# The first adjacency block of the first gather, loaded and multiplied in two column halves

## The reference

```python
def L0(x, adj, W):
    deg = sum(adj, axis=-1, keepdims=True)
    agg = einsum('bij,bjf->bif', adj, x) / maximum(deg, 1e-6)
    return relu(einsum('bnf,of->bno', concatenate([x, agg], 2), W))

def L1(X, A, kernel, bias):
    Ah = A + eye(1024)
    dh = rsqrt(sum(Ah, axis=-1))
    An = dh[:, :, None] * Ah * dh[:, None, :]
    return relu(einsum('bnm,bmf,fc->bnc', An, X, kernel) + bias)

x = layernorm(x + L0(x, adj, L0_gnn_W))
x = layernorm(x + L1(x, adj, L1_gnn_kernel, L1_gnn_bias))
```

## Time and profile before

| | |
|---|---|
| median of three runs | 500.82 us (500.78 to 501.29) |
| the profiled execution | 501.08 us, of which the span from first to last instruction is 499.3 us |
| TensorE busy | 490.4 us, 98% of the span, 2751 matmuls |
| VectorE, ScalarE busy | 393.2 us (79%), 330.6 us (66%) |
| DMA | 93.38 MB, mean 187 GB/s |

### The profile page before, as it was taken

How to read it: one execution, slowest core, us unless ns; L and a number is a source line. 1 busy time by engine, 2 the same in 40 slices (tenths; PEclk the granted TensorE clock), 3 DMA queues, 4 the chain that set the end, 5 groups by cost and what they waited for, 6 DMA issues and landing times.

```text
span 499.3 us, 8174 instructions
## 1 busy us (share of the span) xinstructions
PE 490.4 (98%) x2751; PEld 430.4 (86%) x2751; DVE 393.2 (79%) x963; ACT 330.6 (66%) x614; POOL 2.3 (0%) x8
## 2 busy tenths in 40 slices
PE   8999999999999999999999999999999999999993
PEld 7988888988899888998889988898888988889993
DVE  6787897679966799667996679866898668976755
ACT  6898557765766658756596574965848658477415
POOL 0000000000000000000000000000000000000001
PEclk9999999999999999999999999999999999999998
DMA  8999509762195523936149280593607932051002
GB/s 306 398 376 394 200 1 347 286 210 86 56 376 199 210 84 100 390 140 243 52 155 388 94 287 0 196 393 107 227 0 258 372 120 90 0 211 43 0 1 84
DMA packets 36878, 93.38 MB, mean 187 GB/s; under 512 B 2944, under 2 KB 3840, under 8 KB 36864
## 3 DMA queue, kind: packets, MB, share of 16 engines
q1 hardware_dynamic: 36432, 92.81, 51.1%
q10 hardware_dynamic: 432, 0.39, 0.3%
HBM read 84.80 MB, written 8.39 MB: 187 GB/s over the span
## 4 chain that ended last, share of the span: by engine, by line
PE 97%; ACT 1%; DMA 1%; DVE 0%; POOL 0%; issue 0%; DVEq 0%; ACTq 0%
PE ring_b L890 22%; PE ring_b L892 22%; PE ring_b L891 22%; PE ring_a L890 9%; PE ring_a L892 9%; PE ring_a L891 9%; PE ring_b L936 1%; PE ring_b L945 1%; PE ring_b L949 1%; DMA adj_raw<-adjT 1%; ACT x L381 0%; ACT adj_nat L498 0%; ACT adj_nat L495 0%; POOL x L307 0%; DVE x L678 0%
## 5 line engine op out<-in xcount | busy, mean ns | idle before, releaser
L890 PE MATMUL ring_b<-adj_hi,x1s_hi 128*128 128x512 f32 (+1 forms) x256 | 98.3, 384 | 0.0
L892 PE MATMUL ring_b<-adj_hi,x1s_lo 128*128 128x512 f32 (+1 forms) x256 | 98.0, 383 | 0.0
L891 PE MATMUL ring_b<-adj_lo,x1s_hi 128*128 128x512 f32 (+1 forms) x256 | 97.9, 382 | 0.0
L890 PE MATMUL ring_b<-adj_hi,x_hi 128*128 128x512 f32 x240 | 93.7, 391 | 0.0
L892 PE MATMUL ring_b<-adj_hi,x_lo 128*128 128x512 f32 x240 | 93.5, 390 | 0.0
L891 PE MATMUL ring_b<-adj_lo,x_hi 128*128 128x512 f32 x240 | 93.3, 389 | 0.0
L313 ACT ACTIVATE gath_hi<-ring_b 128x512 fp32r<-128x512 f32 (+1 forms) x64 | 36.5, 583 | 64.5 <-PE ring_b L892 64.5
L547 DVE TENSOR_TENSOR adj_lo<-adj_raw,adj_hi 128x1024 fp32r<-128x1024 f32 (+1 forms) x68 | 76.4, 1158 | 3.1 <-ACT adj_hi L313 3.1
L328 ACT ACTIVATE adj_nat<-adj_nat 128x1024 f32<-128x1024 f32 x64 | 67.2, 1052 | 4.9 <-DMA adj_nat<-adjN 4.6
L313 ACT ACTIVATE adj_hi<-adj_raw 128x1024 fp32r<-128x1024 f32 (+2 forms) x68 | 65.0, 997 | 1.8 <-DMA adj_raw<-adjT 1.7
L547 DVE TENSOR_TENSOR gath_lo<-ring_b,gath_hi 128x512 fp32r<-128x512 f32 (+1 forms) x64 | 42.6, 678 | 21.7 <-ACT gath_hi L313 21.7
(11 more groups left out here) (112 smaller groups left out, 966.2 us busy)
## 6 DMA issues: line engine op xcount, KB each, us to landing
adj_nat<-adjN SPq DMA_DIRECT2D x64, 512.0 KB, 5.8
adj_raw<-adjT SPq DMA_DIRECT2D x60, 512.0 KB, 9.2
out<-x SPq DMA_DIRECT2D x15, 512.0 KB, 3.3
xt_raw<-xT SPq DMA_DIRECT2D x7, 1024.0 KB, 4.8
x_sb<-x SPq DMA_DIRECT2D x14, 512.0 KB, 4.8
adj_raw<-adjT SPq DMA_DIRECT2D x8, 256.0 KB, 5.3
x_sb<-x SPq DMA_DIRECT2D x3, 256.0 KB, 5.3
x<-w SPq DMA_DIRECT2D x2, 256.0 KB, 6.3
```

The costliest lines, as they stand in the source:

```text
L890: nc.tensor.matmul(o, lhi, rhi, start=(first and i == 0), stop=False)
L891: nc.tensor.matmul(o, lhi, rlo, start=False, stop=False)
L892: last = nc.tensor.matmul(o, llo, rhi, start=False, stop=last_part)
```

## The change

The load of piece 0 is cut into a left and a right load of 256 columns each, with a semaphore each. x tile 0 goes from the head of ScalarE's queue to the head of SP's queue. x tiles 2 and 3 (the pair i = 1) go from SP's queue to ScalarE's. On ScalarE the activation table load is issued ahead of its two loads instead of behind them. VectorE casts x tile 0 and forms its remainder first and casts the right half of piece 0 afterwards. PE runs 14 warm-up matmuls; block 0's first two pairs are eight matmuls of 256 columns, four on the left half, then four on the right half, and each side waits for its own rounded half. The start flag is given with the left side's first matmul of each bank only. The pair with a_lo stays at 512 columns.

```diff
--- before.py
+++ after.py
@@ -19,7 +19,7 @@
 NB = 4
 NR = 4
 XP = 2
-WARM = 15
+WARM = 14
 LINE = 128
 HALF = LINE // 8
 PART = (slice(0, NH // 2), slice(NH // 2, NH))
@@ -113,6 +113,7 @@
         x0_loaded = sem("x0_loaded")
         x0_hi_done, x0_lo_done = sem("x0_hi_done"), sem("x0_lo_done")
         adj0_left_hi, adj0_right_hi = sem("adj0_left_hi"), sem("adj0_right_hi")
+        adj0_right_loaded = sem("adj0_right_loaded")
         x_first_hi, x_first_lo = sem("x_first_hi"), sem("x_first_lo")
         adj_first_hi, adj_first_lo = sem("adj_first_hi"), sem("adj_first_lo")
         x_hi_done, x_lo_done = sem("x_hi_done"), sem("x_lo_done")
@@ -227,11 +228,14 @@
                 sp.wait_ge(out_done, b * H + h + 1)
                 sp.dma_start(x_half(out[b], h), x_half(x1, h)).then_inc(x1_free[h], 16)
 
-            sp.dma_start(raw[:, 0, 0, :], adjT[0, 0, 0]).then_inc(raw_first_loaded[0], 16)
+            sp.dma_start(x_sb[:, 0, :], x_first[0]).then_inc(x0_loaded, 16)
+            sp.dma_start(raw[:, 0, 0, 0:NH // 2], adjT[0, 0, 0, :, 0:NH // 2]).then_inc(raw_first_loaded[0], 16)
+            sp.dma_start(raw[:, 0, 0, NH // 2:NH], adjT[0, 0, 0, :, NH // 2:NH]).then_inc(adj0_right_loaded, 16)
             sp.dma_start(raw[:, 0, 1, :], adjT[0, 0, 1]).then_inc(raw_loaded[0][0], 16)
             for i in range(1, CH):
-                loaded = x_first_loaded[i // 2] if i % 2 == 0 else x_loaded[i // 2]
-                sp.dma_start(x_pair(x_sb, i).rearrange("p t c -> p (t c)"), x[0, i]).then_inc(loaded, 16)
+                if i > 1:
+                    loaded = x_first_loaded[i // 2] if i % 2 == 0 else x_loaded[i // 2]
+                    sp.dma_start(x_pair(x_sb, i).rearrange("p t c -> p (t c)"), x[0, i]).then_inc(loaded, 16)
                 sp.dma_start(raw[:, 0, JC * i, :], adjT[0, 0, JC * i]).then_inc(raw_first_loaded[i], 16)
                 sp.dma_start(raw[:, 0, JC * i + 1, :],
                              adjT[0, 0, JC * i + 1]).then_inc(raw_loaded[0][i], 16)
@@ -499,9 +503,9 @@
                                      bias=shift16[:, q:q + 1],
                                      accum_out=moments[:, q, 1:2]).then_inc(act_var_done, 1)
 
-            act.dma_start(x_sb[:, 0, :], x_first[0]).then_inc(x0_loaded, 16)
+            nc.scalar.preload_act_table(ACT.Sqrt)
             act.dma_start(x_sb[:, 1, :], x_first[1]).then_inc(x_first_loaded[0], 16)
-            nc.scalar.preload_act_table(ACT.Sqrt)
+            act.dma_start(x_pair(x_sb, 1).rearrange("p t c -> p (t c)"), x[0, 1]).then_inc(x_loaded[0], 16)
             act.wait_ge(raw_first_loaded[0], 16)
             copy(adj_block(a_hi, 0, 0, 0, NH // 2), raw[:, 0, 0, 0:NH // 2]).then_inc(adj0_left_hi, 1)
             act.wait_ge(x_first_loaded[0], 16)
@@ -830,13 +834,13 @@
             nc.vector.memset(stats[:], 0.0).then_inc(x1_free[0], 16)
             nc.vector.memset(nb[:], 0.0).then_inc(x1_free[1], 16)
             nc.vector.memset(quarter_eps[:], LN_EPS / 4).then_inc(eps_ready, 1)
-            dve.wait_ge(raw_first_loaded[0], 16)
-            nc.vector.tensor_copy(adj_block(a_hi, 0, 0, NH // 2, NH // 2),
-                                  raw[:, 0, 0, NH // 2:NH]).then_inc(adj0_right_hi, 1)
             dve.wait_ge(x0_loaded, 16)
             nc.vector.tensor_copy(x_hi[:, 0, :], x_sb[:, 0, :]).then_inc(x0_hi_done, 1)
             dve.wait_ge(x0_hi_done, 1)
             minus(x_lo[:, 0, :], x_sb[:, 0, :], x_hi[:, 0, :]).then_inc(x0_lo_done, 1)
+            dve.wait_ge(adj0_right_loaded, 16)
+            nc.vector.tensor_copy(adj_block(a_hi, 0, 0, NH // 2, NH // 2),
+                                  raw[:, 0, 0, NH // 2:NH]).then_inc(adj0_right_hi, 1)
             dve.wait_ge(adj0_left_hi, 1)
             dve.wait_ge(adj0_right_hi, 1)
             minus(adj_block(a_lo, 0, 0, 0, NH), raw[:, 0, 0, :],
@@ -922,8 +926,6 @@
                     a_at, x_at = adj_block(a_hi, 0, j, 0, NH), x_hi[:, j, :]
                     if j == 0:
                         pe.wait_ge(x0_hi_done, 1)
-                        pe.wait_ge(adj0_left_hi, 1)
-                        pe.wait_ge(adj0_right_hi, 1)
                     elif j == 1:
                         pe.wait_ge(x_first_hi, 1)
                         pe.wait_ge(adj_hi_done, 1)
@@ -932,18 +934,28 @@
                         pe.wait_ge(adj_first_hi, i)
                     else:
                         pe.wait_ge(adj_hi_done, i + 1)
-                    for f in range(FT):
-                        nc.tensor.matmul(ring_b[:, f, :], x_at[:, f * P:(f + 1) * P], a_at,
-                                         start=(j == 0), stop=False)
                     if j == 0:
-                        pe.wait_ge(x0_lo_done, 1)
-                    elif j == 1:
-                        pe.wait_ge(x_first_lo, 1)
-                    elif j % JC == 0:
-                        pe.wait_ge(x_first_lo if j % TH == 0 else x_lo_done, j // TH + 1)
-                    for f in range(FT):
-                        nc.tensor.matmul(ring_b[:, f, :], x_lo[:, j, f * P:(f + 1) * P], a_at,
-                                         start=False, stop=False)
+                        for i0, side_hi in ((0, adj0_left_hi), (NH // 2, adj0_right_hi)):
+                            side, a_side = slice(i0, i0 + NH // 2), adj_block(a_hi, 0, 0, i0, NH // 2)
+                            pe.wait_ge(side_hi, 1)
+                            for f in range(FT):
+                                nc.tensor.matmul(ring_b[:, f, side], x_at[:, f * P:(f + 1) * P], a_side,
+                                                 start=(i0 == 0), stop=False)
+                            pe.wait_ge(x0_lo_done, 1)
+                            for f in range(FT):
+                                nc.tensor.matmul(ring_b[:, f, side], x_lo[:, 0, f * P:(f + 1) * P], a_side,
+                                                 start=False, stop=False)
+                    else:
+                        for f in range(FT):
+                            nc.tensor.matmul(ring_b[:, f, :], x_at[:, f * P:(f + 1) * P], a_at,
+                                             start=False, stop=False)
+                        if j == 1:
+                            pe.wait_ge(x_first_lo, 1)
+                        elif j % JC == 0:
+                            pe.wait_ge(x_first_lo if j % TH == 0 else x_lo_done, j // TH + 1)
+                        for f in range(FT):
+                            nc.tensor.matmul(ring_b[:, f, :], x_lo[:, j, f * P:(f + 1) * P], a_at,
+                                             start=False, stop=False)
                     pe.wait_ge(adj_first_lo if j % JC == 0 else adj_lo_done, i + 1)
                     for f in range(FT):
                         last = nc.tensor.matmul(ring_b[:, f, :], x_at[:, f * P:(f + 1) * P],
```

## The result

The changed kernel takes 502.06 us (median of 22 runs, 501.0 to 504.65) against 501.0 us of the kernel before (22 runs beside it, 500.48 to 501.64). The ratio is 1.0023, 95% interval 1.0015 to 1.0031. The median hides the shape: of the 22 runs of the changed kernel 11 lie between 501.0 and 501.8 and 11 between 502.3 and 504.7, with none in between. The kernel before has one group.

A forecast was written before the change was run, and what follows sets the result against it. TensorE, busy 98% of the span, was taken as the bound, so changes before block 1 pass to the end. Block 1 at 6.78 instead of 6.96 us gains 0.2 us: 500.6 us, range 500.2 to 501.8.

The forecast's parts named there:

- the same: Whole kernel: a time within about 0.2%, 1.0 us, of the kernel before; chance 0.85.
- the hold by the table load: ScalarE's start: the activation table load might delay the DMA issues behind it, by 0, 1.28 or at most 2.64 us.
- case B: Table load holds ScalarE's DMAs 1.28 us; PE starts at 4.5, block 1 at 6.78; 0.2 us gained, 500.6 us, chance 0.42.
- cases A, B and C: ScalarE's DMAs held not at all, 1.28 us, or up to 2.64 us: 501.2, 500.6, 501.7 us; chances 0.27, 0.42, 0.12.
- case A: No hold; left half shares with the pair's packets, PE starts at 5.6, block 1 at 7.36; 0.4 us lost, chance 0.27.
- the rise fixed at 6.2 us: TensorE's clock, in block 0: goes from the 1.2 to the 2.4 GHz level at about 6.2 us, as before.
- the fourth rival: Before block 0: PE idle from 4.5 to 5.6 us, clock rise slips; 1.4 us lost, 502.2 us, chance 0.07.
- Packet for packet: First loads: the two DMA queues take turns by packet, not by byte, whether packets are 1 KB or 2 KB.
- a saving is handed on one for one to the end: From block 1 on: time saved before it reaches the end in full, unless a later block finds its data missing.

The follow-up runs named there:

- e4: The changed kernel unaltered, timed again for another profile: 502.88 us, ratio 1.0041 to the kernel before, 3 of 3 runs in the upper group (above 502.3 us).
- e9: The kernel before with 10 warm-up matmuls instead of 15 and nothing else: 502.36 us, ratio 1.0026, 4 of 7 runs above 502.3 us.
- e6: The changed kernel with 19 warm-up matmuls instead of 14: 501.33 us, ratio 1.0007 to the kernel before, 0 of 11 runs above 502.3 us.
- e2: The kernel before with only the load of x tiles 2 and 3 moved to ScalarE's queue, ahead of the table load: 501.15 us, ratio 1.0.
- e8: The changed kernel with an extra 8 KB load, read by nothing, at the head of SP's queue: 503.51 us, ratio 1.0047 to the kernel before, two runs.
- e12: The changed kernel with x tiles 0 and 1 on ScalarE's queue, the pair on SP's behind piece 1, and 16 warm-ups: 501.35 us, ratio 1.0006 to before.
- e10: The changed kernel unaltered, timed a third time: 501.5 us, ratio 1.002 to the kernel before, 4 of 12 runs above 502.3 us.
- e5: The changed kernel with piece 1 second on ScalarE's queue and the pair fourth on SP's: 501.4 us, ratio 1.0017 to before, 5 of 12 above 502.3 us.
- e11: The changed kernel with piece 1 on ScalarE's queue, the pair on SP's, and 19 warm-ups: 501.57 us, ratio 1.0013 to before, 1 of 11 above 502.3 us.
- e3: The changed kernel with x tiles 0 and 1 on ScalarE's queue and the pair on SP's behind piece 1: 501.31 us, ratio 1.0007 to the kernel before.
- e7: The kernel before with only x tile 0 moved to the head of SP's queue: 501.45 us, ratio 1.0006.
- e1: The changed kernel with the load of x tiles 2 and 3 back on SP's queue, behind piece 1: 502.04 us, ratio 1.0021 to the kernel before.

## Why the prediction was wrong

The forecast was 500.6 us, with a range of 500.2 to 501.8, and "the same" with 0.85; the measured time is 502.06, above the range, and the difference, 0.23%, lies past the mark of 0.2% by a little. Two steps failed: the hold by the table load, which made case B the forecast, and, for the rest, the sums of cases A, B and C, which fixed the rise at 6.2 us and gave the late issue of piece 1 no cost. The first alone would have left the time inside the range (case A, 501.2).

**The hold by the table load.** The prediction chose case B, a hold of 1.28 us; there is none (DMA issued at 0.77 beside the load that began at 0.74). By the Trainium skill, "PSUM — Partial Sum Buffer", section "Engine vs sequencer instructions", a sequencer waits for dispatch and not for completion; the trace agrees with this row. The drain that the Trainium skill gives in "ScalarE: Activation LUTs", section "What ACT_TABLE_LOAD costs", did not hold the DMAs. It was the row of the old order, in which nothing stood behind the table load, that could not decide it.

**Case A's start of block 0** was put at 5.6 us and measured at 4.89, 5.28 and 4.90. The small loads land sooner than the sum's 2.4 us plus packets: x tile 0 in 2.6, 2.6 and 2.8 us from its issue, where the sum has 3.3. The idle stretch ahead of block 0 is therefore 0.3 to 0.7 us, not 1.1. The halves still gained nothing over the earlier trace rows, since the left half is ready no sooner than the whole piece was.

**The step that failed most** is the rise fixed at 6.2 us, and with it the fourth rival's chance, 0.07: the sentence "a rise may slip after such a stretch" set against "there is no row of such a gap ahead of the rise". In three profiles of the changed kernel the rise came at 4.9, 8.7 and 7.0 us. e4 shows the slip after 0.73 us, e9 shows that the idle time alone makes it, with loads untouched, and e6 that the upper group goes when the idle time is filled. In the changed kernel it and the late piece 1 together put 18 of 37 runs into the upper group. Its size was about right: the prediction gave 1.4 us, and e4's span is 1.4 us longer, from an earlier start but with the low level reaching into block 1. The part of the change that I passed over in one line, one warm-up matmul less, works in the harmful direction when block 0 doesn't start earlier; this is argued, as no run has the changed kernel with 15.

**Piece 1** was to land at 6.25 in case A and to cost nothing. Over the four profiles with its issue at 2.1 us and the pair on ScalarE's queue it landed at 7.4, 5.8, 6.1 and 5.9 (the last is e6). The mean, 6.3, is near the sum; what was missing is the gap, which put it 1.1 us past the sum in one of the four. Piece 1's second place on SP's queue was cover, and the prediction costed its loss at nothing, because "its data are due only after 3.9".

**The gap.** Taking the issue rows of every profile: once ScalarE's loads are in, loads of 256 KB land 0.67 us apart on SP's queue, except for one step (in e2, e8 and e12 ScalarE's loads still fell into it). Beside it stands the longest single packet that began between 2.3 and 9 us, from the list of packets:

| profile | step from one landing to the next, us | longest packet, us |
|---|---|---|
| before, e9, e10 | 1.0 each | 0.77, 0.41, 0.66 |
| e4, e5, e11 | 0.95, 1.1, 1.0 | 0.41, 0.79, 0.88 |
| e2 | 1.2 | 0.40 |
| e6 | none | 0.38 |
| e3, e7 | 1.7, 1.6 | 1.23, 0.71 |
| after, e1 | 2.0, 2.0 | 1.29, 1.12 |
| e8, e12 | 2.7, 2.2 | 1.40, 1.54 |

In the kernel before and in e9 it strikes the fourth load, piece 2, which in the trace of before has over 0.6 us of cover (copied by about 7.65, due at 8.32); in the changed kernel the fourth load is piece 1, which has none, and it was struck in the first profile and by a little in e10, not in e4 and e6. Every step of 2 us or more goes with a packet of more than 1.1 us, and no profile with a step up to 1.2 us has one above 0.9, so a few slow packets seem to make the load late. Why they are slow stays open; e8 was to tell a place in the queue from a moment in time, and fits neither.

**What was right.** Block 2 and later never waited in the changed kernel; the whole loss is made before block 1 (1.23 us of 1.3 in the profile); 2754 matmuls. "Packet for packet" did not hold in the changed kernel, see below. One small slip of the sum: in case B the 34 packets of piece 1 that are left run alone, which at the sum's own 200 packets per us takes 0.17 us and not 0.34; nothing hung on it.

How the loss divides over many runs between the slip and the gap is not settled, since each timed set has one profile: the slip is shown in one profile of three (e4), the late piece 1 in one (the first), neither in one (e10). That e5 keeps its upper group and e6 loses it says that the slip is the larger part. The premise that a saving is handed on one for one to the end is untested in the changed kernel, which saved nothing; in e3 and e7, which did, it failed at 27.8 us.

## What to carry to other kernels

Warm-up work must reach to the first real matmul in the worst execution, not in the profiled one: 0.7 to 1.0 us of idle time ahead of the rise cost 1.4 to 1.8 us in the two profiles that have it, and in the changed kernel about half of the executions lay in the upper group; a surplus matmul costs 0.2 us at most. Of the loads at the head of a queue, the one with the least cover should not be moved back. Before counting on a gain at the start, look for the next load that the faster engine would run into, as at 27.8 us here. Where a change touches the start, look at the spread of the runs: two groups say that something happens in some executions and not in others, and one profile shows one of them.

## What the runs showed of the hardware

- The rise to the high level came at 4.1 to 7.0 us in twelve profiles of fourteen, with PE busy up to then or idle for at most 0.4 us, and it moved by 2 us between two executions of one kernel (4.9 in the first profile of the changed kernel, 7.0 in e10). After 0.73 us of idle time it came at 8.7 (e4), after 0.99 us at about 10.3 (e9).
- After 1.93 us of idle time a granted high level fell back, at 7.5 us, when PE had been at work again for over a microsecond; it was back at 10.9 (e8, one profile).
- The table load of ScalarE, 0.74 to 2.02 us, doesn't hold the DMA issues behind it, which started at 0.77 and 1.20.
- The two queues did not always share packet for packet. From 3.4 to 4.0 us of the changed kernel (packets, MB, share of 16 engines' time) ScalarE's, with the pair of 2 KB packets, moved twice as many as SP's with the halves:

```profile
q10 hardware_dynamic: 95, 0.18, 77.9%
q1 hardware_dynamic: 47, 0.03, 18.0%
```

  e4, e6 and e10 show the same (91, 97 and 103 packets against 56, 52 and 50). Whether SP's queue had a packet ready at every moment the traces don't say.

- A load of 128 KB at the head of SP's queue landed 2.6 to 3.1 us after its issue, in ten profiles. In all profiles but one, one load in the first 9 us landed 0.3 to 2.1 us later than the step of 0.67 us lets expect, and single packets took up to 1.54 us (e12).
